# Row and output slots of an expert loop doubled from four to eight, row loads issued further ahead of the weights

## The reference

```
flat = x.reshape(-1, C)                     # 8192 tokens, C = 64
probs = softmax(flat @ router_w.T)          # 8 experts
topk_probs, topk_idx = top_k(probs, 2)      # normalised to sum to 1
h = silu(flat @ w1[e].T) * (flat @ w3[e].T) # 682 hidden units per expert
y = h @ w2[e].T
out = sum over a token's two experts of gate * y
```

## Time and profile before

| | us |
|---|---|
| median of 3 runs | 1197.35 (1197.1 to 1197.75) |
| the profiled execution | 1195.68 |
| its span, first to last instruction | 1193.9 |
| first up of the expert loop (tile 0) starts at | 523.62 |
| last up of the expert loop (tile 70) starts at | 1149.57 |
| granted TensorE clock, mean over the span | 0.757 |

### The profile page before, as it was taken

One profiled execution on the slowest core, in us unless ns is written; L12 is line 12 of the kernel. 1 busy time (PEld: TensorE's weight loads), 2 busy tenths in 40 slices (PEclk: granted clock), 3 DMA queues, 4 the chain that ended last, 5 costly groups with the idle time before them and its releaser, 6 DMA issues.

```text
span 1193.9 us, 13939 instructions
## 1 busy us (share of the span) xinstructions
PE 782.1 (66%) x4664; PEld 565.4 (47%) x4664; DVE 510.7 (43%) x1246; ACT 335.1 (28%) x605; POOL 363.2 (30%) x353
## 2 busy tenths in 40 slices
PE   3768879677887865046666665666666576666652
PEld 2556667566656553034444443444444344444431
DVE  2565766776575553113233333323332332323233
ACT  0133343242334232022232222223222222322221
POOL 1131234638364455721211221121122112211230
PEclk9567576575757555568897888888888888888885
DMA  1000001000010000422223222322322232223219
GB/s 57 10 1 10 10 1 32 21 26 30 10 34 14 23 20 32 129 86 91 82 81 90 93 80 85 99 81 82 97 88 81 85 99 82 79 81 104 81 34 211
DMA packets 61975, 75.47 MB, mean 63 GB/s; under 512 B 23872, under 2 KB 48480, under 8 KB 61904
## 3 DMA queue, kind: packets, MB, share of 16 engines
q1 hardware_dynamic: 50000, 59.21, 16.9%
q0 software_dynamic: 8640, 12.74, 3.2%
q10 hardware_dynamic: 3264, 2.63, 0.7%
HBM read 58.54 MB, written 16.47 MB: 63 GB/s over the span
## 4 chain that ended last, share of the span: by engine, by line
DMA 27%; issue 25%; POOL 19%; PE 14%; DVE 10%; SPq 3%; ACT 1%; POOLq 1%; DVEq 0%
DMA xin<-expert_rows 12%; DMA expert_results<-yout,xin 12%; POOL expert_rows L472 11%; POOL expert_results L498 6%; PE bk L702 3%; SPq L383 3%; DVE yout L1211 2%; DVE ysum L1207 2%; DVE ysum L1205 2%; PE bk L732 2%; DMA res<-expert_results 2%; PE bk L532 1%; POOL rr L434 1%; PE bk L714 1%; PE bk L610 1%
## 5 line engine op out<-in xcount | busy, mean ns | idle before, releaser
L498 POOL DMA_INDIRECT expert_results<-yout,xin x142 | 139.5, 983 | 505.4 <-DVE yout L1211 474.4
L1200 DVE TENSOR_TENSOR units<-bk,silu 128x512 f32<-128x512 f32 x213 | 147.2, 691 | 285.9 <-ACT silu L878 241.6
L714 PE MATMUL bk<-xs,wbuf 64*128 64x256 f32 x1704 | 222.3, 411 | 1.1 <-ACT xs L865 1.1
L714 PEld LDWEIGHTS bk<-xs,wbuf 64*128 64x128 f32 x1704 | 172.5, 205 | 62.9 <-issue 40.0
L702 PE MATMUL bk<-const,xin 128*128 128x128 f32 x142 | 35.2, 335 | 254.1 <-DMA xin<-expert_rows 254.1
L878 ACT ACTIVATE silu<-bk 128x512 f32<-128x512 f32 x213 | 127.2, 597 | 104.1 <-PE bk L714 72.3
L725 PE MATMUL bk<-units,wbuf 128*64 128x256 f32 x852 | 154.4, 516 | 0.0
L702 PEld LDWEIGHTS bk<-const,xin 128*128 128x128 f32 x142 | 15.6, 153 | 282.1 <-DMA xin<-expert_rows 237.5
L472 POOL DMA_INDIRECT expert_rows<-srow,pos x128 | 131.3, 1026 | 39.6 <-issue 39.6
L865 ACT ACTIVATE xs<-bk 128x256 f32<-128x256 f32 x71 | 27.3, 384 | 254.9 <-PE bk L702 254.9
L725 PEld LDWEIGHTS bk<-units,wbuf 128*64 128x64 f32 x852 | 71.7, 178 | 52.4 <-issue 41.3
(11 more groups left out here) (184 smaller groups left out, 1053.3 us busy)
## 6 DMA issues: line engine op xcount, KB each, us to landing
wbuf<-in_weights SPq DMA_DIRECT2D x71, 576.0 KB, 3.8
xin<-expert_rows SPq DMA_DIRECT2D x71, 130.0 KB, 2.2
res<-expert_results SPq DMA_DIRECT2D x16, 256.0 KB, 4.3
expert_results<-yout,xin POOLq DMA_INDIRECT x142
xg<-in_x SPq DMA_DIRECT2D x8, 256.0 KB
expert_rows<-srow,pos POOLq DMA_INDIRECT x128
out<-og ACTq DMA_DIRECT2D x8, 256.0 KB, 3.0
expert_rows<-const SPq DMA_DIRECT2D x5, 130.0 KB
```

Source lines behind the costliest of these rows:

```text
L498: g.indirect_dma_start(results[:, :], bass.IndirectOffsetOnAxis(ap=xin[:, t % SLOTS, h, ROW - 1:ROW].bitcast(U32), axis=0), yout[:, t % SL ...
L714: last = mm(bank[:, ch * MT:(ch + 1) * MT], wbuf[part, t % SLOTS, at:at + P], xs[part, t % 2, :], start=True, stop=True)
L1200: tt(units[:, t % 2, q, :], h3_ps[q], silu[:, q, :], ALU.mult).then_inc(unit_ready, 1)
```

## The change

The one constant SLOTS is split. Weights keep four slots (W_SLOTS), rows and outputs (xin, yout) and the semaphores xin_loaded and y_scattered get eight (X_SLOTS). SP's order changes with it: weights 0 to 2 come first, then rows 0 to 5, and then weights(t) and rows(t + 3) in turn from t = 3. Rows(t) now wait for the scatters of tile t - 8. All work on the other engines stays as it was, with the new slot numbers. The core of the diff:

```
-SLOTS = 4
+W_SLOTS = 4
+X_SLOTS = 8
...
-        xin = sb("xin", [P, SLOTS, 2, ROW])
-        wbuf = sb("wbuf", [P, SLOTS, CH * P + CH * C])
+        xin = sb("xin", [P, X_SLOTS, 2, ROW])
+        wbuf = sb("wbuf", [P, W_SLOTS, CH * P + CH * C])
...
-        yout = sb("yout", [P, SLOTS, 2, C])
+        yout = sb("yout", [P, X_SLOTS, 2, C])
...
             def load_weights(t):
-                wait(sp, down_done, t - SLOTS + 1)
+                wait(sp, down_done, t - W_SLOTS + 1)
...
             def load_rows(t):
-                wait(sp, y_scattered[t % SLOTS], 32 * (t // SLOTS))
+                wait(sp, y_scattered[t % X_SLOTS], 32 * (t // X_SLOTS))
...
             sp.wait_ge(sched_ready, 1)
-            load_weights(0)
-            load_weights(1)
+            for t in range(W_SLOTS - 1):
+                load_weights(t)
             sp.wait_ge(pads_written, 16 * (NE + 1))
             for b in range(ROW_SLOTS):
                 sp.wait_ge(scattered[b], 2 * NJ * 16 * ((NG - b + ROW_SLOTS - 1) // ROW_SLOTS))
-            load_rows(0)
-            load_rows(1)
-            for t in range(2, NT):
+            for t in range(X_SLOTS - 2):
+                load_rows(t)
+            for t in range(W_SLOTS - 1, NT):
                 load_weights(t)
-                load_rows(t)
-
-            for b in range(SLOTS):
-                sp.wait_ge(y_scattered[b], 32 * ((NT - b + SLOTS - 1) // SLOTS))
+                if t + X_SLOTS - 1 - W_SLOTS < NT:
+                    load_rows(t + X_SLOTS - 1 - W_SLOTS)
+
+            for b in range(X_SLOTS):
+                sp.wait_ge(y_scattered[b], 32 * ((NT - b + X_SLOTS - 1) // X_SLOTS))
```

More of the change, by code:

```diff
@@ L326, in hybrid_block @@
         pads_written = sem("pads_written")
-        xin_loaded = [sem(f"xin_loaded{b}") for b in range(SLOTS)]
-        w_loaded = [sem(f"w_loaded{b}") for b in range(SLOTS)]
-        y_scattered = [sem(f"y_scattered{b}") for b in range(SLOTS)]
+        xin_loaded = [sem(f"xin_loaded{b}") for b in range(X_SLOTS)]
+        w_loaded = [sem(f"w_loaded{b}") for b in range(W_SLOTS)]
+        y_scattered = [sem(f"y_scattered{b}") for b in range(X_SLOTS)]
         xt_turned = sem("xt_turned")
@@ L375, in load_weights @@
             def load_weights(t):
-                wait(sp, down_done, t - SLOTS + 1)
+                wait(sp, down_done, t - W_SLOTS + 1)
                 expert = sp.value_load(tile_expert[t:t + 1, 0:1], min_val=0, max_val=NE - 1)
-                sp.dma_start(wbuf[:, t % SLOTS, :], weights[ds(expert, 1)].rearrange("e p n -> (e p) n"))\
-                    .then_inc(w_loaded[t % SLOTS], 16)
+                sp.dma_start(wbuf[:, t % W_SLOTS, :], weights[ds(expert, 1)].rearrange("e p n -> (e p) n"))\
+                    .then_inc(w_loaded[t % W_SLOTS], 16)
             def load_rows(t):
-                wait(sp, y_scattered[t % SLOTS], 32 * (t // SLOTS))
+                wait(sp, y_scattered[t % X_SLOTS], 32 * (t // X_SLOTS))
                 row = sp.value_load(tile_row[t:t + 1, 0:1], min_val=0, max_val=NE * REG)
-                sp.dma_start(xin[:, t % SLOTS, :, :], rows[ds(row, MT), :].rearrange("(h p) w -> p h w", h=2))\
-                    .then_inc(xin_loaded[t % SLOTS], 16)
+                sp.dma_start(xin[:, t % X_SLOTS, :, :], rows[ds(row, MT), :].rearrange("(h p) w -> p h w", h=2))\
+                    .then_inc(xin_loaded[t % X_SLOTS], 16)
             sp.wait_ge(sched_ready, 1)
-            load_weights(0)
-            load_weights(1)
+            for t in range(W_SLOTS - 1):
+                load_weights(t)
             sp.wait_ge(pads_written, 16 * (NE + 1))
@@ L499, in _ @@
                         results[:, :],
-                        bass.IndirectOffsetOnAxis(ap=xin[:, t % SLOTS, h, ROW - 1:ROW].bitcast(U32), axis=0),
-                        yout[:, t % SLOTS, h, :], None, bounds_check=DUMP - 1, oob_is_err=False)\
-                        .then_inc(y_scattered[t % SLOTS], 16)
+                        bass.IndirectOffsetOnAxis(ap=xin[:, t % X_SLOTS, h, ROW - 1:ROW].bitcast(U32), axis=0),
+                        yout[:, t % X_SLOTS, h, :], None, bounds_check=DUMP - 1, oob_is_err=False)\
+                        .then_inc(y_scattered[t % X_SLOTS], 16)
         @block.tensor
@@ L698, in turn_rows @@
             def turn_rows(t):
-                pe.wait_ge(xin_loaded[t % SLOTS], 16 * (t // SLOTS + 1))
+                pe.wait_ge(xin_loaded[t % X_SLOTS], 16 * (t // X_SLOTS + 1))
                 wait(pe, silu_ready, NU * (t - 1) + 1)
                 for h in range(2):
-                    last = turn(xt_ps[:, h * P:(h + 1) * P], xin[:, t % SLOTS, h, 0:2 * C], ident)
+                    last = turn(xt_ps[:, h * P:(h + 1) * P], xin[:, t % X_SLOTS, h, 0:2 * C], ident)
                 last.then_inc(xt_turned, 1)
@@ L707, in up @@
                     pe.wait_ge(xs_ready, t + 1)
-                    pe.wait_ge(w_loaded[t % SLOTS], 16 * (t // SLOTS + 1))
+                    pe.wait_ge(w_loaded[t % W_SLOTS], 16 * (t // W_SLOTS + 1))
                 wait(pe, unit_ready, NU * (t - 1) + q + 1)
@@ L713, in up @@
                         part = slice(half * C, (half + 1) * C)
-                        last = mm(bank[:, ch * MT:(ch + 1) * MT], wbuf[part, t % SLOTS, at:at + P],
+                        last = mm(bank[:, ch * MT:(ch + 1) * MT], wbuf[part, t % W_SLOTS, at:at + P],
                                   xs[part, t % 2, :], start=True, stop=True)
@@ L724, in down @@
                         at = W2_AT + (2 * q + ch) * C
-                        last = mm(yt_banks[t % 2][ch * C:(ch + 1) * C, 0:MT], wbuf[:, t % SLOTS, at:at + C],
+                        last = mm(yt_banks[t % 2][ch * C:(ch + 1) * C, 0:MT], wbuf[:, t % W_SLOTS, at:at + C],
                                   units[:, t % 2, q, ch * MT:(ch + 1) * MT], start=q == 0, stop=q == NU - 1)
@@ L1208, in gate_out @@
                 dve.wait_ge(ysum_ready, 2 * t + 2)
[L1209 to L1212, removed]
+                dve.wait_ge(xin_loaded[t % X_SLOTS], 16 * (t // X_SLOTS + 1))
+                wait(dve, y_scattered[t % X_SLOTS], 32 * (t // X_SLOTS))
+                tt(yout[:, t % X_SLOTS, :, :], ysum[:, t % 2, :, :],
+                   wide(xin[:, t % X_SLOTS, :, 2 * C], C), ALU.mult).then_inc(yout_ready, 1)
             for t in range(NT):
```

## The result

| | before | changed |
|---|---|---|
| median | 1197.22 us (4 runs) | 908.69 us (4 runs, 908.37 to 909.8) |
| profiled execution, its span | 1195.68, 1193.9 us | 908.37, 906.6 us |
| first up of the loop | 523.62 us | 523.48 us |
| last up of the loop | 1149.57 us | 862.19 us |

The ratio is 0.7596, with a 95% interval of 0.7581 to 0.7611: 24% less time. The prediction was 910.0 us, in a range of 898 to 940.

A forecast was written before the change was run, and what follows sets the result against it. Row loads waiting for scatters of tile t - 4 (9.11 us per tile) bound the kernel; 539.24 to up(3), 67 x 4.82 = 322.9 and 44.3 gave a 906.5 us span, 908.3 executed, 910.0 median; range 898 to 940.

The forecast's parts named there:

- The ring that bound the kernel: Expert loop: row loads wait for scatters of tile t - 4, which wait on earlier rows; one tile per 9.11 us.
- The next limit: Expert loop without the row wait: TensorE's own order sets 4.82 us per iteration; VectorE is 62% busy.
- T: Length of one loop iteration, taken as 4.82 us; between 4.7 and 4.95 with chance 0.72.
- The clock: TensorE's granted clock in the new loop: 1.00 (2.4 GHz) throughout, where the old loop had 0.87.
- Rival A: TensorE's granted clock stays at 0.87: 5.54 us per iteration, median 958 us; chance 0.09.
- Its extreme: TensorE all at 1.2 GHz: 9.04 us per iteration, time 1193 us.
- The start and the end: Up(3) starts at 539.24 us as in the old trace; from up(70) to the end stays 44.3 us.
- The cover of the weights: On SP, weights issued behind a row load that waits for scatters still land 4.2 us before up wants them.
- 4T >= 9.4 + 0.75 + 1.16 + 3.7 = 15.0: SP's order over four iterations: scatter landed, row issue, weight issue, weight landing; alone it would allow T = 3.8 us.
- rival B: Weights landing in 10 us make T = 5.3 and 944 us; sign: TensorE waits for weights at up; chance 0.06.
- Rival C: Slower than before: weights behind waiting row loads take 24 us more, T = 9.75, time 1240 us; chance 0.01.

The follow-up runs named there:

- the shorter down: Kernel with eight slots and the old order of loads, with only 2 of the 6 matmuls of down: 848.92 us, ratio 0.7106.
- the short down: The changed kernel with only 2 of the 6 matmuls of down: 880.67 us, ratio 0.7372.

## Why the prediction was right, point by point

- **The ring that bound the kernel.** Right. Slots alone bring 907.3 us, order alone 1200.5, and the old kernel does not profit from less TensorE work.
- **The next limit and its size.** Right. T = 4.83 against 4.82, from one iteration at the loop's start. That TensorE sets it is shown by the shorter down, which moves the new pace (848.9 us in the old order) and not the old one.
- **The clock.** Right: 1.00 from 528.78 us to 865 us, behind the last up. Rival A did not occur. (Its extreme has a slip: 1197 - 67 x 0.07 is 1192, not 1193.)
- **The start and the end.** Up(3) at 538.59 in place of 539.24; the first up took 4.72 us where it had taken 5.23, because the clock rose earlier in it (0.86 from 527 to 528 us, where it was 0.50 before). The end, 906.6 - 862.2 = 44.4 us, has the predicted 44.3. The sum is now 538.6 + 67 x 4.83 + 44.4 = 906.6 us. That it meets the predicted 906.5 so closely is luck: the loop began 0.65 us early and its iterations took 0.7 us more in all.
- **The cover of the weights.** The mechanism was right and its size off. "4T >= 9.4 + 0.75 + 1.16 + 3.7 = 15.0" took every term from the old loop's start: the scatter's landing of 2.15 us without a load beside it, and the ups at the full clock. Three runs that let this ring bind give 17.1, 16.9 and 17.6 us, but these are not one length. With rows five ahead the surplus is up at the low clock; with rows four ahead it is the late row load behind the scatter. In the changed kernel the clock is full, and what is left is the lateness, which differs from tile to tile. By a ring of 17 us the spare would be some 2 us and not 4.2; at tile 62 it was nothing, and TensorE waited 0.35 us. That is the prediction's own sign of rival B, once in the loop and without weight in the time. With the short down, at T = 4.41, the order chosen in the change binds.
- **Rival C** was called next to impossible for this order, rightly. With rows five ahead the same ring gives away 248 of the 288 us.
- **What the change needs.** Six slots of rows are enough, and the new order of loads brings nothing here. Neither the old order (907.3), six slots (906.8) nor four output slots (907.8) is told apart from the changed kernel; the old order with more slots has the wider cover (weights issued at 700.07 for an up at 708.87, 8.8 us ahead). No run beat the changed kernel with the full computation.

## What to carry to other kernels

When a load waits for a slot and the slot for a store, write the loop of waits down as a ring, count over how many iterations it closes, and compare its length divided by that count with the busiest engine's own iteration: here 9.0 us over one iteration with four slots, 16.7 over three with five, then TensorE's 4.83. With each slot more, follow the ring anew: it need not run through the same steps. In an in-order queue each wait moved forward shortens the ring of all that is issued behind it; more prefetch of the one load can take the other's away. Take transfer times for such a sum with a margin when the new pace will put transfers side by side that were apart before, and if the ring holds a pause of TensorE, take the work behind it at the low clock.

## What the runs showed of the hardware that was not expected

A scatter of 128 rows of 256 bytes landed 2.15 us after its issue in the old loop's chain; in the loop with five slots, at a DMA share of 0.48, it took 2.7 us in the median and up to 5.2, while a row load of 130 KB kept its median of 2.2 us. Taking the weight loads away still left single scatters at 4.05 us at a DMA share of 0.14, so a full set of DMA engines is not the whole cause. That part stays open.
